# The running sum of the weights takes add and bypass with a PSUM bank as its idle operand, and all queues are ordered anew

## What is computed

```python
e = exp(clip(W + K, -20.0, 10.0))
past_attention = cumsum(e * V, axis=1)
past_energy = cumsum(e, axis=1)
eu = exp(clip(U + K, -20.0, 10.0))
A = shift(past_attention) + eu * V
B = shift(past_energy) + eu
out = (sigmoid(R) * (A / B)) @ Wo.T + bo
```

## Time and profile before

| What | Value |
|---|---|
| Median of three timed executions | 1751.92 us (1750.75 to 1754.88) |
| The profiled execution, by its span | 1750.0 us |
| DVE busy | 1523.8 us (87%) |
| PE busy | 1465.9 us (84%) |
| POOL busy | 1300.3 us (74%) |
| ACT busy | 1232.9 us (70%) |

### The profile page before, as it was taken

The page is one execution under the profiler, slowest core; times in us unless marked ns, Lnnn a source line. Parts: engine busy times, 40 slices in busy tenths (PEclk is TensorE's granted clock), DMA queues, the critical chain, the costliest instruction groups (busy, mean ns, idle before and its releaser), DMA issues.

```text
span 1750.0 us, 18988 instructions
## 1 busy us (share of the span) xinstructions
PE 1465.9 (84%) x4800; PEld 713.5 (41%) x4800; DVE 1523.8 (87%) x2045; ACT 1232.9 (70%) x2003; POOL 1300.3 (74%) x970
## 2 busy tenths in 40 slices
PE   4246479779998998898898997999989978999988
PEld 2111224234543553363434452354534542546464
DVE  3399899899999999999999988999999999975571
ACT  3747498947789779858787866977788677655621
POOL 0696996889789886988789867998589887742250
PEclk9667699879999999999899998999999998999999
DMA  8633355334436244354345324453435432311211
GB/s 253 209 110 132 120 173 183 103 118 147 158 106 202 84 133 143 111 188 132 117 138 177 118 68 166 145 202 115 145 103 162 148 111 90 104 49 58 60 37 30
DMA packets 163518, 225.20 MB, mean 129 GB/s; under 512 B 13457, under 2 KB 104082, under 8 KB 163410
## 3 DMA queue, kind: packets, MB, share of 16 engines
...
...
## 4 chain that ended last, share of the span: by engine, by line
PE 23%; DVE 21%; ACT 9%; issue 8%; POOL 4%; DMA 3%; SPq 0%; DVEq 0%; ACTq 0%; POOLq 0%
PE ps_r L1345 15%; DVE ps_d L1220 6%; PE ps_r L1354 6%; DVE bu L1227 3%; ACT L947 2%; POOL bu L905 2%; DMA out_dram<-xk 2%; ACT ps_d L1064 1%; DVE bu L1220 1%; DVE sums L1306 1%; PE ps_y L1396 1%; DMA xr<-x_dram 1%; DVE sums L1312 1%; DVE xk L1186 1%; DVE xc L1212 1%
## 5 line engine op out<-in xcount | busy, mean ns | idle before, releaser
L905 POOL TENSOR_TENSOR bu<-rep,bc 128x512 f32<-128x512 f32 x512 | 663.0, 1325 | 93.9 <-PE ps_y L1396 85.9
L1220 DVE TENSOR_TENSOR_SCAN ps_d<-ps_d,bu 128x512 f32<-128x512 f32 x384 | 457.4, 1214 | 26.4 <-POOL bu L905 15.4
L1064 ACT ACTIVATE ps_d<-rep,scale_a 128x512 f32<-128x512 f32 x512 | 337.6, 683 | 201.6 <-DVE bu L1227 181.0
L1345 PE MATMUL ps_r<-xT,wgu 128*128 128x512 f32 x768 | 352.1, 606 | 30.4 <-ACT hf L1086 8.4
L1345 PE MATMUL ps_r<-mix,wkv 128*128 128x512 f32 x512 | 244.9, 615 | 28.2 <-DVE yr L1327 7.2
L947 ACT ACT_TABLE_LOAD x201 | 257.9, 1283 | 3.6
L1227 DVE TENSOR_TENSOR bu<-ps_d,bc 128x512 f32<-128x512 f32 x384 | 253.7, 676 | 1.2
L1345 PEld LDWEIGHTS ps_r<-xT,wgu 128*128 128x128 f32 x768 | 143.3, 192 | 234.6 <-issue 227.1
L1396 PE MATMUL ps_y<-bu,sel 128*32 128x512 f32 x1024 | 153.2, 673 | 88.0 <-DVE bu L1227 55.1
L910 POOL TENSOR_TENSOR bu<-bu,bc 128x512 f32<-128x512 f32 x128 | 178.0, 1393 | 53.3 <-DVE bu L1220 52.6
L922 POOL TENSOR_TENSOR kv<-sums,kv 128x1024 f32<-128x1024 f32 x64 | 150.7, 2355 | 65.2 <-DVE sums L1312 64.4
...
## 6 DMA issues: line engine op xcount, KB each, us to landing
rep<-dd_scratch SPq DMA_DIRECT2D x128, 512.0 KB, 4.5
...
```

The source lines that it names most:

```text
L905: pool.tensor_tensor(bu[:, i % BU, :], rep[:, g % REP, 1, :], bc[:, 0, q, :], ALU.mult)\
L1064: act.activation(ps_d[D_BANK[i]][:, :], rep[:, g % REP, 0, :], ACT.Exp, scale=scale_a[:, a, NQ * j + q:NQ * j + q + 1]).then_inc(decay_rea ...
L1220: dve.tensor_tensor_scan(states, d[:, :], bu[:, i % BU, :], 0.0, ALU.mult, ALU.add)\
L1345: last = pe.matmul(dst, lhs, rhs, start=n == 0, stop=n == len(pairs) - 1)
```

## The change

`v_esum` no longer multiplies by ones. It adds e to the state (op0 is add) and passes the result on (op1 is bypass). A scan instruction has a second tensor operand in any case; it is now the PSUM bank in which the products of e and V lie. Its values don't enter the result. Since that bank must be written, `v_esum` waits for the products of its own tile, and since `v_evsum` gives the bank free, `v_evsum` waits for `v_esum`.

```diff
                         dve.wait_ge(clipped.sem, at(clipped, r, i + 1))
-                        dve.tensor_tensor_scan(sums[:, 0, 1:], ones[:, 0:1].to_broadcast([P, T]), kv[:, row(i, "e"), :], 0.0,
-                                               ALU.mult, ALU.add).then_inc(e_summed.sem, 1)
+                        unused = ps_r[BANK[r, "p_v", i]]
+                        dve.wait_ge(ev_ready.sem, at(ev_ready, r, 2 * i + 2))
+                        dve.tensor_tensor_scan(sums[:, 0, 1:], kv[:, row(i, "e"), :], unused[:, :], 0.0,
+                                               ALU.add, ALU.bypass).then_inc(e_summed.sem, 1)
                     elif unit == "v_evsum":
-                        dve.wait_ge(ev_ready.sem, at(ev_ready, r, 2 * i + 2))
+                        dve.wait_ge(e_summed.sem, at(e_summed, r, i + 1))
```

```diff
 POOL
-g_dt0 g_dt1 g_dt2 g_bu0 g_bu1 ... g_bu7 g_hc1 g_hc5 g_dt3 g_bu8
+g_dt0 g_dt1 g_bu0 g_dt2 g_bu1 ... g_bu5 g_hc1 g_bu6 g_bu7 g_bu8 g_hc5 g_dt3 g_bu9
 SP
-s_win2 s_win3 fs_ffn0 s_win4 s_win5 s_xc0 s_xc1 fs_ffn1 fs_ffn2
+s_win3 s_xr0 s_wkv2 s_win4 fs_ffn0 s_win5 s_win6 fs_ffn1 s_xc0
```

More of the change, by code:

```diff
@@ L101 @@
     "p": (
[L102 to L136, removed]
@@ new lines @@
+        "hp_turn*2 p_in*5 p_xproj p_in p_dt p_in*2 p_dt*3 p_y hp_turn*2 p_y p_in*4 p_y*5 p_in*2 p_y p_in*2 p_y "
+        "p_xproj p_y p_dt*2 p_y*2 p_dt*2 p_y hp_turn*2 p_y*3 p_post p_y p_post fp_turn p_y fp_turn2 fp_turn "
+        "fp_turn2 p_y fp_gate fp_up fp_gate p_y fp_up fp_gate fp_up fp_gate p_y fp_up fp_gate fp_up p_y fp_gate "
+        "fp_up p_y fp_down fp_down2 p_y fp_down fp_down2 p_in*5 p_y p_in fp_turn p_y fp_turn2 fp_turn fp_turn2 "
+        "p_in*2 p_xproj p_k p_dt p_recept p_y p_recept*3 p_y p_recept*3 p_v p_k*2 p_v p_dt*2 p_y p_v p_dt "
@@ new lines @@
+        "p_recept p_k p_y p_v p_k p_y p_k p_v*2 hp_turn p_y p_k p_wo p_wo2 p_y p_post*2 p_wo p_y p_v p_wo2 "
+        "fp_turn fp_turn2 fp_turn fp_turn2 fp_gate fp_up p_y fp_gate fp_up fp_gate fp_up fp_gate fp_up p_y "
+        "fp_gate fp_up fp_gate fp_up p_k p_v p_y fp_down fp_down2 fp_down fp_down2 hp_turn p_y p_in*2 p_wo "
+        "fp_turn fp_turn2 p_wo2 fp_turn fp_turn2 p_in p_y p_in*2 p_wo p_wo2 p_in*3 p_y p_xproj p_k p_v p_dt "
+        "rp_turn rp_turn2 rp_turn rp_turn2 p_y p_recept rp_gate rp_up rp_gate rp_up rp_gate rp_up rp_gate p_y "
@@ new lines @@
+        "rp_up p_dt p_y rp_gate*2 rp_up*2 p_y p_k rp_down rp_down2 rp_down p_y rp_down2 p_v p_y p_recept*2 p_k*2 "
+        "p_v*2 p_recept p_y p_recept*3 p_k p_v p_k p_recept p_y p_dt p_k p_v p_post*2 p_v p_wo p_wo2 fp_turn "
+        "fp_turn2 p_y fp_turn fp_turn2 p_wo p_wo2 fp_gate fp_up fp_gate p_y fp_up fp_gate fp_up fp_gate fp_up "
+        "fp_gate fp_up p_y fp_gate fp_up p_k p_dt p_y p_v fp_down fp_down2 fp_down fp_down2 hp_turn*2 p_y p_wo "
+        "p_wo2 p_wo fp_turn fp_turn2 fp_turn fp_turn2 p_wo2 p_in*2 p_k p_y*2 p_in rp_turn rp_turn2 rp_turn "
@@ new lines @@
+        "rp_turn2 p_in*2 p_v p_in*3 p_y p_xproj p_dt p_k p_y p_recept*3 p_v p_k p_v p_dt p_y rp_gate rp_up "
+        "p_recept p_y rp_gate rp_up p_k p_v p_recept rp_gate rp_up p_y p_recept rp_gate rp_up rp_gate rp_up p_y "
+        "rp_gate p_recept rp_up p_k p_y rp_down p_v p_recept rp_down2 rp_down p_y rp_down2 p_k p_v p_y p_wo p_k "
+        "p_wo2 p_post*2 p_y p_v p_wo p_wo2 p_dt fp_turn fp_turn2 fp_turn fp_turn2 p_k fp_gate*2 fp_up*2 p_y "
+        "fp_gate fp_up fp_gate fp_up p_y fp_gate fp_up p_dt p_y p_v fp_gate fp_up p_y fp_down fp_down2 fp_down "
@@ new lines @@
+        "fp_gate fp_up fp_gate fp_up fp_gate p_v fp_up p_wo p_y p_wo2 fp_gate*2 fp_up*2 p_k p_y p_v fp_down "
+        "fp_down2 fp_down p_dt fp_down2 p_y p_dt p_wo p_wo2 p_y p_wo p_wo2 fp_turn fp_turn2 fp_turn fp_turn2 "
+        "hp_turn*2 p_k p_in rp_turn p_in rp_turn2 p_v rp_turn rp_turn2 p_in*2 p_recept p_in*2 p_xproj p_y p_dt*2 "
+        "p_in p_y p_in p_k p_y p_recept*2 p_v p_dt p_y rp_gate rp_up p_k rp_gate rp_up p_v p_recept rp_gate rp_up "
+        "p_k p_y p_recept p_v rp_gate rp_up rp_gate*2 p_y rp_up*2 p_recept*2 p_y rp_down rp_down2 rp_down "
@@ new lines @@
+        "rp_up p_recept rp_gate rp_up p_k p_v p_y rp_gate p_recept rp_up rp_gate rp_up rp_gate rp_up p_recept p_y "
+        "rp_down rp_down2 rp_down rp_down2 p_y p_recept p_k*2 p_dt p_y p_v*2 p_recept p_y p_wo p_k p_wo2 p_post*2 "
+        "p_wo p_wo2 p_y p_v fp_turn fp_turn2 fp_turn fp_turn2 p_k p_y p_v fp_gate fp_up fp_gate fp_up fp_gate "
+        "fp_up p_y fp_gate fp_up fp_gate*2 fp_up*2 p_dt fp_down p_y p_wo p_wo2 p_wo p_wo2 fp_down2 fp_down "
+        "fp_down2 p_y fp_turn rp_turn p_y fp_turn2 fp_turn fp_turn2 rp_turn2 rp_turn p_y rp_turn2 p_k p_y "
```

459 lines of the change are left out of this document (232 added, 227 removed), and 120 rows, old and new, of tables (BANKS, ORDER).

## The result

The changed kernel takes 1724.12 us in the median of 4 executions (1718.89 to 1725.72), the kernel before 1751.34 (1745.77 to 1754.88). The ratio is 0.9842, 95% interval 0.9820 to 0.9864: faster by 27 us, where I had forecast 11. Three further sets of executions gave it 1724.89, 1724.50 and 1724.41 us, ratios 0.9860 [0.9834, 0.9886], 0.9823 [0.9802, 0.9845] and 0.9842 [0.9811, 0.9873]. The direction and the scan's new length came as predicted. The time ended at the rival that I had given the least chance, "the lists also meet better" (1722).

The account below looks back on a forecast made before the run. DVE, 95% busy in the middle stretch, was taken to set the pace. 1750.0 - 6.5 (scans) - 1.0 (POOL) + 1.2 (neighbours) - 5.0 (start) = 1738.7 us of span, forecast as 1740.5 us timed; own range 1732 to 1748, 8-in-10 range 1722 to 1757.

Parts of the forecast that it names:

- the lists also meet better: Rival: new lists also remove about a quarter more of DVE's idle time in the middle, 18 us; 1722 us, chance 0.10.
- The scan's length: Each sum of e on DVE falls from a mean of 1330 ns to 1199 ns, none over 1.25 us.
- Its worth: Shorter sums of e in DVE's middle stretch, 50 scans from 66.48 to 59.95 us: 6.5 us less.
- about the same idle time: Sign: DVE's middle stretch gets some 9 us shorter, while its idle time there, 69.8 us, stays about the same.
- the last stretch: From the last state-space scan to the end: same 116 PE units, left at about 227 us, no gain.
- The first wait, of 5.25 us: DVE's wait for POOL ahead of the first state-space scan at 73.89 us; the scan comes earlier by up to 5.25 us.
- Nothing arrives: Rival: new lists lose elsewhere what start and scans give, 81 instead of 70 idle DVE us in the middle; 1751 us, chance 0.11.
- The start: Up to the first state-space scan: reordered POOL and SP lists save 2 and 3 us, 5 together, between 0 and 9.3.
- the two exchanges that it names: At the start, POOL's `g_bu0` moves ahead of `g_dt2` (2 us) and SP's `s_win4` ahead of `fs_ffn0` (3 us).
- The neighbours: DVE units right behind the one they wait for cost 0.11 us a pair; 65 pairs become 76, +1.2 us.
- The filler: Rival: in 17 tiles, 12 in the middle, the sum of e no longer covers DVE's wait for PE; 1762 us, chance 0.13.
- POOL's relief: POOL's L905, no longer held by DVE, falls from 1325 to some 1290 ns: 1 us off the path, between 0 and 5.6.

Follow-up runs that it names:

- old_lists_47_scans: The kernel before, lists unchanged, with the new form of the sum of e in 47 tiles and the old form in 17: 1750.39 us, ratio 0.9990.
- old_lists_new_scan: The kernel before with the new scan and its two waits, the sum of e moved behind the products in 17 tiles: 1759.66 us, ratio 1.0039.
- old_lists_moved: The kernel before, old scan kept, with the sum of e moved behind the products of e and V in 17 tiles: 1762.17 us, ratio 1.0057.

## Why the prediction was right in direction and too small

**The scan's length: right.** 1213 ns in the mean and nothing over 1224 against a forecast of about 1200 and nothing over 1250; in the middle 49 of them take 59.4 us where 50 were to take 59.95. By the Trainium skill (VectorE: DVE Perf Modes, The TRN2 errata) it would have been an estimated 1281 ns, 62 cycles more for the PSUM source. The measurement decides: 1214 ns in the median with an operand in PSUM, 1216 without. The rule of the Trainium skill that two inputs in SBUF contend with a GpSimd instruction that reads SBUF (SBUF — State Buffer, Who interferes with whom) holds here, by 12 scans held before and none after; the runs add that an operand that is passed over counts as an input.

**Its worth: right for the old lists, wrong for the new.** I priced the scans by how often they were held before, 6.5 us. That is the price in the old order, and even there the neighbours ate most of it. In the new order the scans of the old form take 23 us more. The two halves of the change aren't addends: the lists alone brought 5 us (0.9971), the scan alone at most some 6 (`old_lists_47_scans`, interval 0.9967 to 1.0013), both together 27.

**The step that failed** is in the sum: it has no term for the lists' own effect on the waits behind the start ("about the same idle time" in the middle, and "the last stretch [...] I leave it as it is"). Both were put at nothing, and they gave 11.2 and 4.9 us, 16.1 of the 26.1. The argument, that DVE's waits are spread over dozens of places and a new list makes new ones, was a reason not to foresee the sum, not a reason for zero. The places are many, 28 waits in the profile before, but 30.5 us stood ahead of one line, L1220, of which 5.25 at the start, and that is what shrank, to 13.5. One row of the groups would have shown where new lists had something to win. In the last stretch the argument was that the same 116 PE units follow. It says that PE's work stays, and it did; but PE idled there for 21.2 us, and that could shrink.

**Smaller faults in the working.** The first wait, of 5.25 us, ends the first stretch; the prediction counts it among the 69.8 idle us of the middle. The signs that it gives, a first scan 7 to 9 us earlier and a middle some 9 us shorter, make 16 to 18 us together, not the 11.3 of its own sum. And its bounds, all taken at one end, give 1729 to 1754 us; the 1732 to 1748 isn't worked out from them. "Nothing arrives" is excluded: it needed 81 idle us in the middle, and there are 58.6.

**The start: right in size, and partly by luck.** The first scan came 7.7 us earlier (3.8 in the profile with the lower clock), for which 7 to 9 were forecast, and 4.3 us of it were kept by 131 us (0.1 in that other profile), for which the sum has 5.0. But the two exchanges that it names are worth 8.8 us in the new lists and 1.9 in the old ones, at the first scan. That the rest of the lists takes from them or adds to them was no part of the forecast.

**The neighbours: right in price for two sums, too low for the others.** 0.12 us for a pair of the two sums, as read from the earlier trace rows. But behind its `v_ev` the changed scan starts 0.13 us after the end (median of 16 pairs) and not 0.03, so these pairs cost 0.22 each. With 16 of them and 13 pairs of sums the term is some 4 us, an estimate from the gaps of the two traces, in place of 1.2. In `old_lists_new_scan` it was 9.7 us (6.6 and 3.1), nearly all of the 11.7 that the scans gave.

**The filler: not here.** L1297 waits for PE 5.8 us against 5.5. In the old lists `old_lists_moved` lost 10 us by 17 tiles, half of the 22 us that I had put on twelve, but its profile doesn't show the wait either, so the filler stays open there.

**POOL's relief: right.** L905's mean was to be 1290 and is 1297, and in `old_lists_47_scans`, where it comes with the scans alone, nothing of it shows at the end.
